# One output tile scattered on TensorE instead of two in a routed-expert kernel

## The reference

```python
x = x + tanh(g_xattn) * attention(layernorm(x), ctx)        # 16 heads, causal, 256 keys
# mixture of experts, on n = layernorm(x), 512 tokens of 256
logits = n @ router_weight.T                                 # 64 experts
topw, topi = top_k(softmax(logits), 8); topw /= topw.sum(-1)
pos = running count of the token's expert over all (token, choice) pairs
xe[e, pos] = n[token]            # 64 experts, capacity 128, later ones dropped
h  = silu(xe @ gate[e]) * (xe @ up[e])                       # 96 wide
ye = h @ down[e]                                             # 128 x 256 per expert
y[token] = sum over its 8 choices of topw * ye[choice, pos]  # 0 where pos >= 128
x = x + tanh(g_ffn) * y
```

## Time and profile before

| | us |
|---|---|
| median of three executions | 231.3 (230.06 to 232.07) |
| profiled execution | 230.18 |
| its span, first to last instruction | 228.1 |
| PE busy | 208.7 (91%) |
| DVE, ACT, POOL busy | 144.6, 110.7, 108.5 |

### The profile page before, as it was taken

How to read it: one execution, slowest core, us unless ns; L and a number is a source line. 1 busy time by engine, 2 the same in 40 slices (tenths; PEclk the granted TensorE clock), 3 DMA queues, 4 the chain that set the end, 5 groups by cost and what they waited for, 6 DMA issues and landing times.

```text
span 228.1 us, 5260 instructions
## 1 busy us (share of the span) xinstructions
PE 208.7 (91%) x1678; PEld 171.4 (75%) x1678; DVE 144.6 (63%) x466; ACT 110.7 (49%) x350; POOL 108.5 (48%) x146
## 2 busy tenths in 40 slices
PE   8789999999999568699899899899899999999983
PEld 3457767777555257599899899789799899999972
DVE  6366354575697828645665765665667566658795
ACT  2526445425526625345465564555456666445531
POOL 7201222312255454755666566655666650765720
PEclk9999999999999979979999999999999999999999
DMA  5599999999020242768888989888865562223222
GB/s 153 184 299 287 306 280 262 245 238 206 8 75 29 65 117 84 183 180 239 264 241 245 257 252 282 226 266 260 243 164 168 168 162 93 72 78 98 81 46 92
DMA packets 37726, 41.04 MB, mean 180 GB/s; under 512 B 3874, under 2 KB 35044, under 8 KB 37700
## 3 DMA queue, kind: packets, MB, share of 16 engines
q1 hardware_dynamic: 32932, 27.21, 42.8%
q0 software_dynamic: 4048, 12.98, 21.9%
q10 hardware_dynamic: 720, 0.52, 0.8%
HBM read 32.97 MB, written 7.74 MB: 178 GB/s over the span
## 4 chain that ended last, share of the span: by engine, by line
PE 77%; DVE 8%; DMA 7%; issue 4%; ACT 2%; ACTq 0%; POOL 0%; DVEq 0%; POOLq 0%
PE bank L753 15%; PE scores L769 12%; PE scores L742 9%; PE bank L742 9%; PE scores L732 6%; PE bank L537 5%; PE bank L552 4%; PE scores L518 3%; PE bank L775 3%; DMA gate_w<-in_ctx_dram 3%; PE bank L481 2%; DMA xn<-xn_dram,slot_token 2%; PE bank L500 2%; DMA xe<-xn_dram,slot_token 2%; PE scores L513 2%
## 5 line engine op out<-in xcount | busy, mean ns | idle before, releaser
L460 POOL DMA_INDIRECT gate_w<-xn_dram,slot_token x56 | 58.8, 1049 | 36.2 <-issue 17.6
L753 PE MATMUL bank<-y_high,scatter 128*128 128x256 f32 x156 | 48.6, 337 | 1.5 <-DVE y_low L1271 0.9
L955 ACT ACTIVATE work<-scores,gate_w 128x256 f32<-128x256 f32 x56 | 26.5, 473 | 41.2 <-PE scores L769 30.7
L769 PE MATMUL scores<-down_all,work 96*128 96x256 f32 x128 | 39.5, 390 | 2.7 <-ACT work L962 2.2
L753 PE MATMUL bank<-y_low,scatter 128*128 128x256 f32 x156 | 40.1, 283 | 0.0
L423 POOL TENSOR_SCALAR_AFFINE_SELECT gate_w<-gate_w 128x256 f32<-128x256 f32 x32 | 12.3, 409 | 44.3 <-ACT gate_w L866 44.3
L1266 DVE TENSOR_SCALAR scatter<-tokens,slot_token 128x256 fp32r<-128x256 f32 (+1 forms) x64 | 25.1, 392 | 11.4 <-PE bank L753 10.5
L753 PEld LDWEIGHTS bank<-y_high,scatter 128*128 128x128 f32 x156 | 29.8, 191 | 2.4 <-issue 2.2
L1269 DVE CAST y_high<-work 128x256 fp32r<-128x256 f32 x64 | 20.8, 325 | 16.4 <-ACT work L955 11.2
L753 PEld LDWEIGHTS bank<-y_low,scatter 128*128 128x128 f32 x156 | 29.9, 192 | 0.0
L942 ACT COPY work<-scores 128x256 f32<-128x256 f32 x64 | 23.9, 374 | 10.2 <-PE scores L732 7.8
(11 more groups left out here) (187 smaller groups left out, 320.7 us busy)
## 6 DMA issues: line engine op xcount, KB each, us to landing
ye_dram<-work SPq DMA_DIRECT2D x50, 128.0 KB
gate_w<-_L_ffn_gate_up_proj_dram SPq DMA_DIRECT2D x8, 768.0 KB, 10.7
down_all<-in_L_ffn_down_proj_dram SPq DMA_DIRECT2D x16, 384.0 KB, 9.5
gate_w<-_L_ffn_gate_up_proj_dram SPq DMA_DIRECT2D x32, 192.0 KB
gate_w<-xn_dram,slot_token POOLq DMA_INDIRECT x56
x_sb<-in_x_dram SPq DMA_DIRECT2D x2, 256.0 KB, 4.8
xe<-in_L_xattn_Wq_dram SPq DMA_DIRECT2D x1, 256.0 KB, 3.9
xe<-in_L_xattn_Wout_dram SPq DMA_DIRECT2D x1, 256.0 KB, 6.2
```

Of the source, the lines that this page charges most:

```text
L460: pool.indirect_dma_start(out=rows, out_offset=None, in_=xn2_dram, in_offset=bass.IndirectOffsetOnAxis(ap=slot_token[:, e:e + 1], axis=0), ...
L753: last = nc.tensor.matmul(bank[6 + t // 2][:, t % 2 * H:t % 2 * H + H], scatter[e % 2][:, t * P:t * P + P], (y_high, y_low)[part][e % 2][: ...
L769: nc.tensor.matmul(y_bank(e)[:, 0:H], hT[e % 2], down_w[:, e, :], start=True, stop=True).then_inc(y_mm, 1)
L955: nc.scalar.activation(y_sb[e % Y_RING], y_bank(e)[:, 0:H], ACT.Copy, scale=weight_of(e)).then_inc(y_done, 1)
```

## The change

- `SHARED` 2 to 1 and `EARLY` 50 to 48: only tile 0 is always scattered on PE; tiles 1 to 3 of the first 48 experts go by `ye_dram`, with 24 row gathers and additions instead of 16. The last 16 experts scatter four tiles.
- `FIRST_FOUND` 5 to 6: six searches ahead of the loop, the others in steps 0 to 2; the ranked search moves back a step in DVE (steps 2 to 6) and PE (steps 5 and 6).
- PE's step does `turn_hidden(s - 1)` right behind `gate_up_of(s)`, ahead of the scatter and down; ACT copies hT ahead of y.
- Results are written over the token rows of their expert (`y_of`); the ring `y_sb` goes, and with it ACT's wait for stores. Row gathers land in the token rows of experts 8 to 31.
- From expert 48 on ACT writes the high part straight from PSUM, and DVE computes the low part from PSUM.
- Spreads start later for the early experts (`spread_in`), weight loads are spread over 42 steps, DVE normalises tile 3 instead of POOL, and row gathers are allowed two per step from step 52's neighbourhood on.

```diff
-Y_RING = 4
-EARLY = 50
-SHARED = 2
+EARLY = 48
+SHARED = 1
-FIRST_FOUND = 5
+FIRST_FOUND = 6
-LATE_FROM = 2
+LATE_FROM = 1
+SPREAD_FROM = 0 if SHARED else EARLY
...
+        def y_of(e):
+
+            return xe_of(e)[0][:, 0:H]
+
         def row_of(c):
 
-            at = (E - XE_SEMS) * XW + c * H
-            return used_gates[:, at:at + H], used_up(at + H)
+            assert XE_SEMS + c < EARLY
+            return xe_of(XE_SEMS + c)[0][:, 0:H]
...
         def found_in(s):
 
-            return (FIRST_FOUND + s - 1,) if 1 <= s <= SINGLES - FIRST_FOUND else ()
+            return (FIRST_FOUND + s,) if 0 <= s < SINGLES - FIRST_FOUND else ()
 
         def spread_in(e):
 
-            return e + (4 if e < 8 else 3 if e < 16 else 2)
+            return e + max(2, 6 - e // 6)
...
             for e in range(EARLY):
                 sp.wait_ge(y_done, e + 1)
-                sp.dma_start(ye_dram[e * CAP:e * CAP + CAP, :], y_sb[e % Y_RING]).then_inc(y_out[e % Y_RING], 16)
-                late = RESERVED + e - LATE_FROM
-                if RESERVED <= late < E:
+                sp.dma_start(ye_dram[e * CAP:e * CAP + CAP, :], y_of(e)).then_inc(y_out, 16)
+                for late in range(RESERVED, E):
+                    if e != LATE_FROM + (late - RESERVED) * 4 // 3:
+                        continue
...
-            for r in range(Y_RING):
-                pool.wait_ge(y_out[r], 16 * len(range(r, EARLY, Y_RING)))
+            pool.wait_ge(y_out, 16 * EARLY)
             pool.wait_ge(rows_ready, 1)
             for c in range(ROWS):
-                rows, free_after = row_of(c)
-                pool.wait_ge(gu_mm, max(free_after, min(E, ROWS_FROM + 2 * c // 3)))
+                pool.wait_ge(gu_mm, min(E, ROWS_FROM + c // 2))
                 pool.indirect_dma_start(
-                    out=rows, out_offset=None, in_=ye_dram,
+                    out=row_of(c), out_offset=None, in_=ye_dram,
...
             for e in range(FIRST_FOUND):
                 find_slots(e)
-                if e + 1 < FIRST_FOUND:
-                    stay_warm(bank[4], 2)
+                stay_warm(bank[4], 2)
             find_ranked(0)
+            stay_warm(bank[4], 2)
...
-                for e in range(E):
+                if 0 <= s - 1 < E:
+                    turn_hidden(s - 1)
+                for e in range(SPREAD_FROM, E):
                     if scattered_in(e) == s and s < E:
                         if e == EARLY:
                             pe.wait_ge(all_slots, 1)
                         scatter_of(e)
                 if 0 <= s - 2 < E:
                     down_of(s - 2)
-                if 0 <= s - 1 < E:
-                    turn_hidden(s - 1)
                 for e in found_in(s):
                     find_slots(e)
-                if s in (4, 5):
-                    find_ranked(s - 2)
+                if s in (5, 6):
+                    find_ranked(s - 3)
...
-                if 0 <= s - 2 < E:
-                    e = s - 2
-                    act.wait_ge(y_mm, e + 1)
-                    if e >= Y_RING:
-                        act.wait_ge(y_low_done, e - Y_RING + 1)
-                        act.wait_ge(y_out[e % Y_RING], 16 * min(e // Y_RING, len(range(e % Y_RING, EARLY, Y_RING))))
-                    nc.scalar.activation(y_sb[e % Y_RING], y_bank(e)[:, 0:H], ACT.Copy,
-                                         scale=weight_of(e)).then_inc(y_done, 1)
                 if 0 <= s - 1 < E:
                     e = s - 1
                     act.wait_ge(hid_turned, e + 1)
                     if e >= 2:
                         act.wait_ge(y_mm, e - 1)
                     copy(hT[e % 2], bank[5][0:I, 0:P]).then_inc(hT_done, 1)
...
+                if 0 <= s - 2 < E:
+                    e = s - 2
+                    act.wait_ge(y_mm, e + 1)
+                    if e < EARLY:
+                        nc.scalar.activation(y_of(e), y_bank(e)[:, 0:H], ACT.Copy,
+                                             scale=weight_of(e)).then_inc(y_done, 1)
+                    else:
+                        if spread_nth(e) > 2:
+                            act.wait_ge(scattered, spread_nth(e - 2))
+                        nc.scalar.activation(y_high[e % 2][:], y_bank(e)[:, 0:H], ACT.Copy,
+                                             scale=weight_of(e)).then_inc(y_high_act, 1)
...
+            normalise(3, (TILES - 1,), xn2_done)
             place(1)
...
+            mark_slots(FIRST_FOUND)
             for s in range(E + 3):
                 if s < E:
                     hide(s)
...
-                elif s == 5:
+                elif s == 6:
                     read_ranked()
...
+                    else:
+                        dve.wait_ge(y_high_act, e - EARLY + 1)
+                        v.scalar_tensor_tensor(out=y_low[e % 2][:], in0=y_bank(e)[:, 0:H], scalar=weight_of(e),
+                                               in1=y_high[e % 2][:].bitcast(F32), op0=ALU.mult,
+                                               op1=ALU.subtract).then_inc(y_low_done, 1)
                 for c in range(ROWS):
-                    if s == min(E + 2, ROWS_FROM + 2 * c // 3 + 3):
+                    if s == min(E + 2, ROWS_FROM + 5 * c // 9 + 3):
                         add_row(c)
```

More of the change, by code:

```diff
@@ L174, in flamingo_moe @@
         hT = [take(P, parts=I) for _ in range(2)]
-        take(2816 - 2688)
+        take(2816 - 1664)
         rp = take(TILES * E).rearrange("p (t e) -> p t e", t=TILES)
@@ L362, in _ @@
                     load_gate(late, 1, gate_w_late_in[(late - RESERVED) // CHUNK])
[L363 to L366, removed]
+            for t in range(1 if SHARED else 0, TILES, 2):
+                sp.wait_ge(out_dve, t - SHARED + 1)
+                sp.dma_start(out_tiles[:, t, :], xn[:, t, :]).then_inc(stored, 16)
             sp.wait_ge(stored, 16 * TILES)
@@ L438, in _ @@
             pool.wait_ge(rstd_done, 4)
-            for t in range(QT, TILES):
-                pool.tensor_scalar(xn[:, t, :], x_sb[:, t, :], mv[:, t, 0:1], rstd[:, t:t + 1],
-                                   ALU.subtract, ALU.mult).then_inc(xn2_pool, 1)
+            t = QT
+            pool.tensor_scalar(xn[:, t, :], x_sb[:, t, :], mv[:, t, 0:1], rstd[:, t:t + 1],
+                               ALU.subtract, ALU.mult).then_inc(xn2_pool, 1)
             pool.wait_ge(share_done, 1)
@@ L756, in scatter_of @@
                                                 stop=(e == E - 1 and part == 1), skip_group_check=True)
-                    if e == E - 1 and t == SHARED - 1:
-                        last.then_inc(shared_done, 1)
+                    if e == E - 1 and t == 1:
+                        last.then_inc(first_pair_done, 1)
                 last.then_inc(scattered, 1)
@@ L962, in _ @@
                     copy(hT[e % 2], bank[5][0:I, 0:P]).then_inc(hT_done, 1)
-            act.wait_ge(shared_done, 1)
-            for t in range(SHARED):
-                copy(xn[:, t, :], bank[6][:, t * H:t * H + H]).then_inc(out_act, 1)
-            act.wait_ge(out_act, 2)
-            act.dma_start(out_tiles[:, 1, :], xn[:, 1, :]).then_inc(stored, 16)
-            act.wait_ge(out_dve, 2)
-            act.dma_start(out_tiles[:, SHARED + 1, :], xn[:, SHARED + 1, :]).then_inc(stored, 16)
+                if 0 <= s - 2 < E:
[9 more added lines that the diff above has]
+                                             scale=weight_of(e)).then_inc(y_high_act, 1)
+            for t in range(0 if SHARED else 1, TILES, 2):
+                if t < SHARED:
+                    act.wait_ge(out_dve, 1)
+                    copy(xn[:, t, :], bank[6][:, t * H:t * H + H]).then_inc(out_act, 1)
+                    act.wait_ge(out_act, 1)
+                else:
+                    act.wait_ge(out_dve, t - SHARED + 1)
+                act.dma_start(out_tiles[:, t, :], xn[:, t, :]).then_inc(stored, 16)
         @block.vector
@@ L1166, in add_row @@
                 dve.wait_ge(row_in[c], 16)
-                then(v.tensor_tensor(x_sb[:, t, :], x_sb[:, t, :], row_of(c)[0], ALU.add))
+                then(v.tensor_tensor(x_sb[:, t, :], x_sb[:, t, :], row_of(c), ALU.add))
             for i in range(QUADS):
@@ L1259, in _ @@
                     find_rows()
-                for e in range(E):
+                for e in range(SPREAD_FROM, E):
                     if spread_in(e) != s:
                         continue
-                    if e >= 2:
-                        dve.wait_ge(scattered, e - 1)
+                    if spread_nth(e) > 2:
+                        dve.wait_ge(scattered, spread_nth(e - 2))
                     wide = SHARED * P if e < EARLY else TILES * P
```

65 lines of the change are left out of this document (35 added, 30 removed).

## The result

The kernel after takes 241.21 us (median of four executions, 240.13 to 244.59) against 231.16 for the kernel before beside it: a ratio of 1.042 (95% interval 1.037 to 1.046). One of the four, 244.59, was over 1.5% above the fastest, and the ratio leaves it out. It is slower by 4.2%; the prediction was 223.9 and 86% sure of faster. But this is half of the result. On another chip the same two kernels stand the other way round, at 0.956 (0.947 to 0.965). The runs trace both halves to one thing: how long PE's signals to the other engines take while POOL gathers. A signal here is the raising of a semaphore, by which an instruction tells other engines that it is done.

The account below looks back on a forecast made before the run. PE's issue, with some stalls, was taken to bound the kernel. Gains of 1.2 at the start and 7.1 in the loop, less 0.9 for rows, took 7.4 us off 231.3: 223.9, range 217.5 to 229.5.

Parts of the forecast that it names:

- late signals: In the expert loop, PE's signals reaching ACT late: 12 expected showing about 0.5 us each, 6.0 us in all.
- products transposed first: In each loop step, hid's transpose moves behind gate_up: slack falls from 2.0 to 0.7 us, stalls become 7.2 for 5.2.
- the rows: 24 row gathers at the end: last lands 35 us after step 52 starts; cost 0.9 us, bounds 0.4 and 3.
- the start: Before step 9: earlier searches release gathers sooner, gather 9 at 94.1, step 9 at 102.3; gain 1.2 us, bounds -1 and +4.
- Steps 9 to 54: Expert loop: 76.9 us of PE work plus 7.2 of stalls (bounds 0 and 15), 84.1 against 91.19; gain 7.1 us.
- rival B: Loop: chain gate_up, silu, hide, transpose takes over, each late signal costing 1.2 us; 15 us stalls, 231.7, no change; chance 0.1.
- 88 matmuls, 10.4 us of PE: Scatter on PE: 312 matmuls become 224, all saving on the path; a step falls from 1.89 to 1.655 us.
- rival D: Start: first stall stays, gather 9 lands after 100.5 because the ranked search moved back; gain gone, 226.1; chance 0.15.
- The prediction's other price: Landing of a row gather by the skill's fit: 2.3 us for 128 KB; cost 0.4 and time 0.5 lower.
- Rival C: End: POOL's queue of row gathers; spacing from 1.67 us eats the gain, at 2.03 costs 15.6, 239.5; chance 0.05.
- rival A: Loop: late signals are absorbed, PE's issue binds with 1 us of stalls; 6.2 us lower, 217.7; chance 0.2.

Follow-up runs that it names:

- the paced two-tile kernel: Kernel after with two scattered tiles, 50 early experts and 16 row gathers at the kernel before's pace: 221.21 us (0.988) on chip 11, 220.16 (0.984) on chip 15.

## Why the prediction was wrong

The step that failed is the pricing of the late signals, in the section on the products transposed first, and their absence from the price of the rows. The prediction saw them (silu 2.14 us after its gate_up, ACT idle, PE alone to wait for), gave them a rate in time, one in 7 us, and a cost of 0.5 us each by slack, and never asked what makes them. They were a constant of the loop in the sum. They are made by POOL's gathers, most of all where these follow within 0.8 us, and the change raises just that: a shorter step with one gather each leaves POOL less room, and 24 row gathers are let through two per step.

Of the span, 220.7 was forecast and 239.5 measured. The 18.8 us between are 1.6 at the start, 7.2 in steps 9 to 54, 6.8 in steps 54 to 63 and 3.2 behind the last gate_up.

- **Steps 9 to 54**: PE's own 76.9 us, and 7.2 of stalls, 84.1. Measured 91.34 where signals are held: stalls of 14.4, twice the value taken and just inside its bound of 15. The count was near, 16 late silus for 12, the cost of each was not. That is rival B's price; its mechanism, less slack in the chain from gate_up to the transpose, isn't, for the old order changes nothing (87.53 for steps 9 to 52, where the kernel after takes 86.60 and 89.05). Where none are held, 78.4 (98.20 to 176.56).
- **88 matmuls, 10.4 us of PE; 1.655 a step**: right. Most of the gain shows on chip 11, 86.0 to 78.4 for these steps, though 1.5 less of it than PE's own 76.9 would give.
- **Steps 54 to 63**: no late signal was priced here, since POOL's queue was counted only for when it ends. The stretch takes 28.06 us against 21.25 in the kernel before, and 21.1 in either kernel on chip 11. These 6.8 us are nearly as much as the miss in the loop, and here the price was nothing.
- **The start**: gain 1.2 forecast by way of gather 9 at 94.1. It came at 97.37 in the result's profile, and step 9 at 103.86, 0.4 late: rival D's case (on chip 9, where signals are held too, step 9 came at 99.86, so this stall varies). D's reason, the ranked search moved back, is not what did it, for with the same order gather 9 came at 92.20 on chip 11. In the result's profile the clock was also at its lower level from 84.10 to 90.80, behind idle times of PE of 2.48 and 1.74 us, where the kernel before had 82.30 to 85.70; the forecast has no term for that. On chip 11 step 9 started at 98.20, against 103.34 before: 5.1 us gained, more than the bound of 4. That the clock falls behind the stall for gather 9 was right in the result and on chip 11: gate_up matmuls behind it take 0.53 us where they take 0.33 at the full clock. On chip 9 it did not fall there but at 107.04, three steps on.
- **The rows**: 1.31 apart, the last landing 35 us after step 52 starts. On chip 11 they did: 171.82 to 207.8 is 36. The end there (after on chip 11, DVE and POOL):

```profile
203.87 1.01 POOL L479 DMA_INDIRECT gate_w<-ye_dram,row  x1 [0.30 <-issue]
204.15 1.79 DVE L1180 TENSOR_TENSOR x_sb<-x_sb,gate_w 128x256 f32<-128x256 f32 x4
206.54 0.43 DVE L1180 TENSOR_TENSOR x_sb<-x_sb,gate_w 128x256 f32<-128x256 f32 x1 [0.59 <-DMA gate_w<-ye_dram,row]
207.82 0.43 DVE L1180 TENSOR_TENSOR x_sb<-x_sb,gate_w 128x256 f32<-128x256 f32 x1 [0.85 <-DMA gate_w<-ye_dram,row]
208.28 1.08 DVE L1299 TENSOR_TENSOR xn<-bank,x_sb 128x256 f32<-128x256 f32 x3
```

  DVE waits for the last two rows, and from the last gate_up to the end it is 15.1 us (197.70 to 212.8) against 12.2 before: 2.9 lost, at the upper bound of 0.4 to 3 and not at the 0.9 taken. The last row lands 3.9 after its issue, so the 4.0 of the trace was the right price for it; the median of the 24 is 3.0 there and 3.5 in the result's profile. The prediction's other price, an estimate of 2.3, rests on the fit that the Trainium skill ("DMA: Bandwidth & Descriptors", Anatomy of one DMA) gives for DMAs issued from GpSimd. These gathers are such DMAs, and the medians just given lie 0.7 us and more above it. The plain DMAs of the same size from SP's queue, which that fit is not for, landed in 2.1.
- **Rival C** gave 239.5, 1.7 from the result, by POOL's queue at the end. That the number is near is luck. The place is right, the mechanism not: it needed spacings of 1.67, and they are 1.31 in runs of eight, four, six and six, with pauses of 1.1 to 1.6 between; the mean, (224.80 - 190.74)/23, is 1.48. What cost the time is what these runs do to the others.
- **The sum on a chip without holds** closes: 5.1 at the start, 7.6 in steps 9 to 54, 0 behind, less 2.9 at the end, is 9.8; the spans are 222.6 and 212.8. The ratio of 0.956 is better than the 0.968 forecast (223.9 to 231.3), between it and rival A.

Open remains why signals were held in some sets and not in others (only chip 11 served in two, alike, so that it is the chip is likely and not shown), by what path a gather holds them, and whether recording has a part in it; whether it is the gathers' distance or their number; whether memsets between gathers help where signals are held; and whether the paced two-tile kernel does there. No kernel beat both on every chip: after is the quickest that does the whole work where none are held, and where they are, of those tried there, the kernel before is.

## What to carry to other kernels

When a wait ends late and the profile names as its releaser an instruction long done, find out what else ran at each such moment (here, sorting by what POOL was doing) before giving it a price, because the change may feed that very thing. POOL's indirect gathers are not free for the other engines on every chip: in these profiles nearly no silu was late behind 0.8 us or more of pause, and none where the rows came by plain DMAs. So issue fewer or space them out beside a loop with tight signals, and send what has fixed addresses by a plain DMA. That spacing alone helps was not tested. And measure a change on a second chip: the same pair of kernels gave +4% in the result and on chip 9, and -4% on chip 11.

## What the runs showed of the hardware

- PE's signals were held on two of four chips, and in the result's two profiles, while POOL's indirect gathers followed within 0.8 us of each other. In the kernel after they were recorded up to 3.9 us behind the end of the last matmul that raises them, and a silu started up to 3.8 us beyond its due time. ACT's and DVE's signals were never late: 0 of 2023 recorded, against 777 of 1796 of PE's.
- In these profiles part of the signal records is missing, 322 of 712 in steps 9 to 63 of the kernel after, and none in the 26 us of the kernel with plain row DMAs in which POOL does nothing (144 of 144 stand).
- It seems to sustain itself, as I read the timelines: a held signal holds POOL's own gate too, then two or three gates open at once and the gathers go out in a bunch, 0.30 apart, which holds the next signals. With gates that open 3.3 us apart (chip 9, half the gathers) no bunch formed. No run tested this by itself.
- The same binary of the kernel before takes 223.7 to 225.0 us on chips 11 and 15 and 229.8 to 232.4 on 3 and 9. In steps 9 to 54 the difference is 5.2 us (91.19 in the first trace and 86.00 on chip 11, which is PE's own time).
- An indirect gather of 128 rows of 1 KB took 3.0 us (chip 11), 3.5 and 4.0 us (the result's profiles) in the median to land, a plain DMA of as many bytes 2.1 to 2.2.
